# One behind the other: mixing the two sequences of a chunk on VectorE in a fused language-model tower

## The reference

```
q, k, v = x @ Wq + bq,  x @ Wk + bk,  x @ Wv + bv
Q, K    = elu(q) + 1,   elu(k) + 1
KV      = sum over the sequence of K * v        # one number per sequence and feature
Ksum    = sum over the sequence of K            # the same
V       = Q * KV / (Q * Ksum + 1e-6)            # "mix" in the kernel
a       = gelu(gelu(V @ Wo + bo))
x       = ln1(a + x)
x       = ln2(gelu(gelu(x @ W1 + b1) @ W2 + b2) + x)
```

## Time and profile before

| what | value |
|---|---|
| median of 3 runs | 1213.73 us (1212.25 to 1214.63) |
| profiled execution, own time | 1216.03 us |
| its span | 1214.4 us |
| PE busy | 1036.7 us (85%) |
| DVE busy | 814.9 us (67%) |
| ACT busy | 576.1 us (47%) |
| POOL busy | 346.3 us (29%) |
| reciprocal L1372, 16 times | 104.8 us, 6553 ns each |

### The profile page before, as it was taken

One profiled execution on the slowest core, in us unless ns is written; L12 is line 12 of the kernel. 1 busy time (PEld: TensorE's weight loads), 2 busy tenths in 40 slices (PEclk: granted clock), 3 DMA queues, 4 the chain that ended last, 5 costly groups with the idle time before them and its releaser, 6 DMA issues. The chain is left out here.

```text
span 1214.4 us, 17197 instructions
## 1 busy us (share of the span) xinstructions
PE 1036.7 (85%) x5274; PEld 799.6 (66%) x5274; DVE 814.9 (67%) x2128; ACT 576.1 (47%) x941; POOL 346.3 (29%) x324
## 2 busy tenths in 40 slices
PE   4877999999999999999999988868878768888872
PEld 3665878778778778787778866535535435476661
DVE  2678778887887888779978954657797566332221
ACT  2543644664466346645654534645756532043441
POOL 6223101020102101111300011340007673557774
PEclk9988999999999999999999979879998888898996
DMA  5300101220122111202520000676433224279997
GB/s 129 122 1 1 48 9 70 100 96 1 48 74 69 69 61 48 74 22 82 201 96 1 19 1 4 131 150 114 83 54 111 63 92 177 79 176 179 180 238 120
DMA packets 58454, 103.08 MB, mean 85 GB/s; under 512 B 10858, under 2 KB 38214, under 8 KB 58123
## 3 DMA queue, kind: packets, MB, share of 16 engines
q1 hardware_dynamic: 39227, 59.29, 18.5%
q0 software_dynamic: 19152, 42.92, 13.7%
HBM read 58.59 MB, written 53.00 MB: 92 GB/s over the span
## 5 line engine op out<-in xcount | busy, mean ns | idle before, releaser
L590 PE MATMUL b_ring<-left 128*128 128x256 f32 x960 | 212.1, 379 | 0.0
L590 PEld LDWEIGHTS b_ring<-left 128*128 128x128 f32 x960 | 181.4, 190 | 24.2
L1154 POOL TENSOR_TENSOR b_rstd<-b_veps,b_mhalf 128x4 f32<-128x4 f32 x31 | 34.5, 1112 | 389.1 <-DVE b_veps L1234 389.1
L896 ACT ACTIVATE left<-b_ring,b_cur 128x512 f32<-128x512 f32 x128 | 88.3, 690 | 40.9 <-PE b_ring L580 19.2
L1372 DVE RECIPROCAL b_mixing<-b_mixing 128x1024 f32<-128x1024 f32 x16 | 104.8, 6553 | 0.5
L1860 POOL DMA_INDIRECT xe<-m_row,m_idx x84 | 83.1, 989 | 46.2 <-issue 28.2
L575 PE MATMUL b_ring<-right_rounded,b_mixing_rounded 128*128 128x512 f32 x240 | 95.7, 399 | 0.6 <-ACTq L898 0.6
L2176 ACT ACTIVATE a_ET<-a_pB 128x512 f32<-128x512 f32 x128 | 74.1, 595 | 45.1 <-PE a_pB L1926 43.9
L2204 DVE TENSOR_REDUCE nmax<-a_pA 128x2 f32<-128x512 f32 x112 | 74.4, 688 | 30.6 <-PE a_pA L1902 29.2
L576 PE MATMUL b_ring<-right_rounded,left_rounded 128*128 128x512 f32 x240 | 94.7, 395 | 0.0
L893 ACT ACTIVATE b_ffo<-b_ffo 128x512 f32<-128x512 f32 x32 | 20.1, 629 | 151.7 <-DVE b_ffo L1280 151.7
(11 more groups left out here) (360 smaller groups left out, 2282.7 us busy)
## 6 DMA issues: line engine op xcount, KB each, us to landing
xe<-b_nil POOLq DMA_DIRECT2D x16, 1284.0 KB, 5.6
a_ET<-xe SPq DMA_DIRECT2D x32, 321.0 KB, 4.1
left<-in_w SPq DMA_DIRECT2D x8, 1024.0 KB, 5.7
x_wt<-in_wexp SPq DMA_DIRECT2D x16, 384.0 KB, 4.6
b_wqkv<-in_wqkv SPq DMA_DIRECT2D x4, 768.0 KB, 4.6
b_rows<-in_rows SPq DMA_DIRECT2D x8, 384.0 KB, 4.3
right<-qparts SPq DMA_DIRECT2D x16, 192.0 KB, 4.8
left<-qparts SPq DMA_DIRECT2D x16, 192.0 KB, 5.2
```

Source lines behind the costliest of these rows:

```text
L590: last = pe.matmul(bank[:, j * D:(j + 1) * D], src[:, k, tile], weights[:, k, :], start=(k == 0), stop=(k == n_k - 1))
L896: act.activation(H[:, f, :], bank[:, :], ACT.Gelu_apprx_tanh, bias=col("b1", f)).then_inc(s_h, 1)
```

## The change

VectorE does the denominator, the reciprocal and the products of the first sequence (`b` = 0, both feature halves), raises `s_mix`, and then does the same for the second sequence. The reciprocal of 128x1024 becomes two of 128x512. `s_mix` is raised twice in a step, and TensorE waits for the first raise ahead of pair 0 and for the second ahead of pair 1. Two more links stand in VectorE's chain in each step, and the counts follow.

```diff
-                pe.wait_ge(s_mix, NC * l + s + 1)
                 for pair in range(KD):
+                    pe.wait_ge(s_mix, 2 * (NC * l + s) + pair + 1)
                     rows_product(pair, KD, mix, wo)
...
-                before = sum(3 * ln1(x) + 3 * ln2(x) + 5 * (x < ITEMS) for x in range(s))
-                return before + 11 * NC * l
+                before = sum(3 * ln1(x) + 3 * ln2(x) + 7 * (x < ITEMS) for x in range(s))
+                return before + 13 * NC * l
...
-                for m in range(KD):
-                    for b in range(2):
-                        o = slice(b * SEQ, (b + 1) * SEQ)
+                for b in range(2):
+                    o = slice(b * SEQ, (b + 1) * SEQ)
+                    for m in range(KD):
                         dve.scalar_tensor_tensor(vv[:, m, o], K[:, m, o], 1.0, vv[:, m, o], ALU.mult, ALU.mult,
                                                  accum_out=kv[:, 2 * m + b:2 * m + b + 1])
                         last = dve.tensor_scalar(den[:, m, o], Q[:, m, o], ksum[:, 2 * m + b:2 * m + b + 1], 1e-6,
                                                  ALU.mult, ALU.add)
-                chain.link(last)
-                chain.link(dve.reciprocal(rec, den))
-                for m in range(KD):
-                    for b in range(2):
-                        o = slice(b * SEQ, (b + 1) * SEQ)
+                    chain.link(last)
+                    chain.link(dve.reciprocal(rec[:, :, o], den[:, :, o]))
+                    for m in range(KD):
                         last = dve.scalar_tensor_tensor(mix[:, m, o], Q[:, m, o], kv[:, 2 * m + b:2 * m + b + 1],
                                                         rec[:, m, o], ALU.mult, ALU.mult)
-                last.then_inc(s_mix, 1)
+                    last.then_inc(s_mix, 1)
```

More of the change, by code:

```diff
@@ L1370, in body @@
                                                  ALU.mult, ALU.add)
-                chain.link(last)
-                chain.link(dve.reciprocal(rec, den))
-                for m in range(KD):
-                    for b in range(2):
-                        o = slice(b * SEQ, (b + 1) * SEQ)
+                    chain.link(last)
+                    chain.link(dve.reciprocal(rec[:, :, o], den[:, :, o]))
+                    for m in range(KD):
                         last = dve.scalar_tensor_tensor(mix[:, m, o], Q[:, m, o], kv[:, 2 * m + b:2 * m + b + 1],
                                                         rec[:, m, o], ALU.mult, ALU.mult)
-                last.then_inc(s_mix, 1)
+                    last.then_inc(s_mix, 1)
                 chain.n += 1
                 dve.sem_inc(s_dve, 1)
-                want = 3 * ln1(s) + 3 * ln2(s) + 5
+                want = 3 * ln1(s) + 3 * ln2(s) + 7
                 assert chain.n == want, (s, chain.n, want)
```

## The result

The kernel with the change takes 1197.25 us (median of 4 runs, 1194.21 to 1200.76) beside 1214.03 us for the kernel before (4 runs, 1212.25 to 1214.63). The ratio is 0.9865, with a 95% interval of 0.9833 to 0.9897: by the ratio 16.4 us faster, the interval reaching from 12.5 to 20.3.

A forecast was written before the change was run, and what follows sets the result against it. The prediction took PE's own work to bound the steps, its waits being what could be won. -12.2 (loop) - 1.4 (step 1) + 0.3 (end) = -13.3 us, from 1213.73 to 1200.4; range 1197.5 to 1206.5.

The forecast's parts named there:

- What a wait costs: Output product, steps 2 to 13: each wait for the mixing costs PE 0.26 more than shown; 12.2 us in all.
- When the sequences are ready: VectorE's mixing: first raise 5.6 us after the denominators start, second 0.30 later; neither pair waits, pair 1 having 0.53 to spare.
- E: How much later than in the kernel before the second raise comes; 0.30 us predicted, break-even at 1.72.
- What follows behind: Behind the output product: bias sums, double gelu and next norm move by PE's whole 1.00; about half in three steps.
- rival B: In each step the wait moves to `x1_low` at L580, growing by 1.00; 1212.6 us, chance 0.06.
- Rival A: In the loop part of the gain comes back, leaving half of it; 1206.5 us, chance 0.09.
- Rival C: VectorE's halved reciprocal runs below full rate, so pair 1 waits; 1224.4 us if a third slower, chance 0.05.
- Step 1: Output product of step 1: pair 0 at the upper clock, pair 1 after the clock fell; 1.4 us gained.
- the variant in which the clock holds: Step 1: the clock stays up, pair 1 takes 1.73 and the gain is 3.0 us; 1198.8 us in all.
- The end: Behind step 15: PE's late products wait for DVE, so DVE's added 0.30 is lost once; 0.3 us.
- The sum: Whole kernel: the loop's 12.2 and step 1's 1.4 gained, 0.3 lost at the end; 13.3 us faster.

The follow-up runs named there:

- e6: The changed kernel plus six more VectorE operations on a 128x256 slice ahead of the second reciprocal, results unused; 1217.7 us, ratio 1.0063 to the kernel before.
- e4: The kernel before with the change made in step 1 only, the other steps mixing as before; 1210.55 us, ratio 0.9964.
- e1: The changed kernel run again, unaltered; 1199.4 us, ratio 0.988 to the kernel before.
- e5: The changed kernel plus two more VectorE operations on a 128x256 slice ahead of the second reciprocal, results unused; 1202.75 us, ratio 0.9932 to the kernel before.
- e7: The changed kernel with VectorE doing `x1_low` ahead of the second norm's statistics instead of behind them; 1196.45 us, ratio 0.9892 to the kernel before.

## Why the prediction was right, step by step

**What a wait costs.** Right. Twelve steps at 1.00 plus 0.02 each were to give 12.2. Steps 3 to 13, eleven of the twelve, gave 11.40, 1.036 each; step 2 can't be told apart from step 1's clock. Taking the idle time as shown would have given 9.1. e6 shows the same 0.26 from the other side (0.89 shown, 1.16 lost). What I did not count: the same cost without any row for it. Steps 14 and 15 of before show no wait, but their product takes 3.72, and the change gave 0.28 there.

**When the sequences are ready.** Right: first raise 5.61 (5.6 predicted), reciprocal 3.353 (3.35), second raise 0.31 later (0.30), slack 0.52 (0.53). The fixed part of a reciprocal is 2 x 3353 - 6553 = 153 ns (0.14). Without a price for a link, E would have been 0.153 + 0.04, about 0.19, and it measured 0.31. The Trainium skill, page "VectorE: DVE Perf Modes", section "The DRAIN you can't avoid", says that the semaphore costs nothing extra; the rows hold 0.12 a link against that. The section also says that a next instruction that isn't held starts earlier; with that the rows agree, by 0.09. The section of the Trainium skill on the TRN2 errata, on that page, has every instruction pay a fixed part, and the rows agree. The prediction's estimate of 0.06 took the 58 cycles of its table, which by the Trainium skill's own words below the table are too few for a single instruction; with the about 150 cycles that stand there as measured the estimate would have been 0.16, and the rows show 0.153.

**What follows behind.** Right. The wait at L580 is 10.6 in 14 waits before and after, so rival B is out: the chain to `x1_low` hangs on PE's q products (10.49 and 10.51 to the wait). Rival A is out, since the steps gave no part back. Rival C fell with 3353 ns, and e6 shows that its price in the loop was right: at E = 1.89 a step is 0.12 longer than before, and the kernel is slower.

**Step 1.** The size was nearly right (1.25 against 1.4), the way there was not, so that this term is right by luck. The order of times was as I had it: the product's halves 5.52 apart (5.54 predicted), the wait gone from 7.49 to 2.16 and 1.84. But I let the clock fall 3.8 us into an idle stretch, as in before, and so gave pair 0 the upper level and pair 1 the lower. The granted clock fell from 0.99 to 0.50 when PE had stood 2.2 us and had just begun again (before, it fell in the middle of the stand); pair 0 ran at 1.2 GHz, pair 1 mostly at 2.4, and then the down half paid. e4 reached 2.97, the gain that I gave the variant in which the clock holds, by still another way: pair 0 slow there too, and all behind it at the upper level.

**The end.** Predicted +0.3. The steps are 13.93 shorter at step 15's down half and 13.48 at `first_sum` of step 16, so 0.45 is lost. DVE's 0.31 would explain most, and that the 0.15 that PE gained in step 15's own product doesn't reach DVE, which is ahead of it, would fit the rest; no run tests either.

**The sum.** 13.3 predicted for the stretch that is changed, 13.5 measured, twice. By parts that is 11.40 for steps 3 to 13 (11.2 predicted), 2.25 for steps 1 and 2 (2.4), 0.28 for steps 14 and 15 (nothing), and 0.45 lost at the end (0.3). That the sum is closer than some of its parts is luck.

The medians show 16.4 [12.5, 20.3] and, in e1, 14.6 [9.7, 19.4]: both intervals hold 13.5. The median of 1197.25 is 3.2 below the forecast and just below its range. The term that was too small is the 1 us that the range allowed for the run: the four runs of after lie 6.5 apart, the 23 runs of before on one chip 14. As the gain of the steps recurs to 0.01, the rest of the difference is to be looked for ahead of step 0's product and behind the steps. Profiles with the new order on VectorE have from 511.7 to 520.4 behind the steps, those with the old order from 517.8 to 519.0. I found no cause that links this to the change and don't claim one; with one profile of each kernel a small share can't be excluded.

## What to carry to other kernels

Where PE is the bound and waits a little in every step for a chain of another engine, split the chain's last part by what the consumer reads first: half of the data early is enough if the consumer's work on it covers the rest, and the price on the producer (0.31 us here) is free as long as the second half has slack. Work out that slack and the break-even before building; here the slack held to 0.01 us, and the loss beyond the break-even to 0.05. Count a wait by the delay of the next instruction and not by its idle row: here each cost 0.26 more than shown, and a group of 16 matmuls that took 3.72 in place of 3.62 betrayed waits that had no row at all.

## What the runs showed of the hardware that was not expected

The length of the stand just before doesn't by itself say whether the clock falls in step 1. Ahead of pair 0 PE stood for about 2.2 us in after, e1 and e5, and the clock fell as pair 0 began; it stood for 2.14 in e6, and there pair 0 ran at the upper level throughout. PE's timeline of e6, pair 0 of step 1:

```profile
110.59 2.00 PE L590 MATMUL b_ring<-b_wo,right 128*128 128x256 f32 x8 [2.14 <-DVE right L1378]
```

and the window in which it runs, with the granted clock (1.00) behind the five busy shares:

```profile
111.00:112.00 1.00, 1.00 (x7) 0.87 (x6) 1.00 (x6) 0.00 (x0) 0.00 (x0) 1.00 0.00 0
```

In e4 and e7, where PE had stood for 2.9, the clock also fell as pair 0 began. In after and e1 it fell a second time while PE was busy; in e4 and e7 it did not. That alone is worth 1.7 us between e4 and after (2.97 and 1.25), whose products start at the same times. There is one profile of each kernel, and only after and e1 show the same kernel twice (with the same course). The runs don't say what decides it, and a term of this kind is better given with both ends.

Taking away a wait of 0.8 on DVE brought up another of 0.5 behind it, on ACT's freeing of a bank (e7: 15 times, 7.2 us in all); before shows that wait once, 0.6 in step 1, and after not at all.
